# Row normalisation in a context attention pass: from VectorE to ScalarE, in slot 2 of a turn's last group

## The reference

```
def _layernorm(x, axis=-1, eps=1e-05):
    m = jnp.mean(x, axis=axis, keepdims=True)
    v = jnp.var(x, axis=axis, keepdims=True)
    return (x - m) / jnp.sqrt(v + eps)
...
q = _split_heads(Q @ Wq.T + bq, N_HEAD)          # Q = _layernorm(x); 512 rows, 16 heads of 32
k = _split_heads(K @ Wk.T + bk, N_HEAD)          # K = V = the context, 77 rows
score = jnp.einsum('bhqd,bhkd->bhqk', q, k) / jnp.sqrt(jnp.float32(d_k))
attn = jax.nn.softmax(score, axis=-1)
out = jnp.einsum('bhqk,bhkd->bhqd', attn, v)
...
x = x + jnp.tanh(g_xattn[1]) * (out @ Wo.T + bo)
```

## Time and profile before

| what | value |
|---|---|
| median of 3 runs | 2726.01 us (2723.91 to 2733.47) |
| the profiled execution | 2719.8 us, span 2718.0 us |
| mean granted TensorE clock of it | 0.944 |
| busy over the span: PE, DVE, ACT, POOL | 2356.2 (87%), 1419.5 (52%), 1028.4 (38%), 599.7 (22%) us |
| context attention pass in the span | about 1612 to 2024 us |
| one turn in its middle | 45.6 us |

### The profile page before, as it was taken

The page is one execution under the profiler, slowest core; times in us unless marked ns, Lnnn a source line. Parts: engine busy times, 40 slices in busy tenths (PEclk is TensorE's granted clock), DMA queues, the critical chain, the costliest instruction groups (busy, mean ns, idle before and its releaser), DMA issues. The chain is left out here.

```text
span 2718.0 us, 40799 instructions
## 1 busy us (share of the span) xinstructions
PE 2356.2 (87%) x16348; PEld 1549.0 (57%) x16348; DVE 1419.5 (52%) x1733; ACT 1028.4 (38%) x1185; POOL 599.7 (22%) x204
## 2 busy tenths in 40 slices
PE   7259999999999984799999857999968999999978
PEld 6235555555555542445444325666646888888756
DVE  4345565565565543567777647787745222222124
ACT  3324454454444441355555533444423111111111
POOL 0004654545554562000000002232320000000000
PEclk9679999999999986999999978999988999999989
DMA  7701011011010004111111021122224111111166
GB/s 239 181 33 38 16 46 41 11 44 31 24 45 10 14 13 132 32 48 58 51 46 47 17 86 53 67 83 70 68 93 144 42 44 44 45 44 48 45 234 261
DMA packets 104571, 182.56 MB, mean 67 GB/s; under 512 B 17252, under 2 KB 39780, under 8 KB 99358
## 3 DMA queue, kind: packets, MB, share of 16 engines
q1 hardware_dynamic: 100110, 172.84, 19.2%
q10 hardware_dynamic: 4368, 8.39, 0.8%
HBM read 122.07 MB, written 59.15 MB: 67 GB/s over the span
## 5 line engine op out<-in xcount | busy, mean ns | idle before, releaser
L976 DVE TENSOR_REDUCE att_mx<-att_sn 128x2 f32<-128x1024 f32 x256 | 313.6, 1225 | 169.1 <-PE att_sn L821 166.3
L733 POOL TENSOR_TENSOR att_es<-att_es,att_num 128x2048 f32<-128x2048 f32 x64 | 292.7, 4574 | 15.6 <-ACT att_num L904 9.3
L904 ACT ACTIVATE att_num<-att_st 128x2048 f32<-128x2048 f32 x128 | 240.6, 1879 | 141.0 <-PE att_st L809 81.0
L729 POOL TENSOR_TENSOR att_es<-att_num 128x2048 f32<-128x2048 f32 x32 | 145.9, 4559 | 370.7 <-PE att_pj L791 340.8
L2290 ACT ACTIVATE rec_ga<-rec_g,rec_bg 128x512 f32<-128x512 f32 x84 | 57.2, 689 | 312.0 <-PE rec_g L2189 312.0
L821 PE MATMUL att_sn<-att_kh,att_qh 32*128 32x512 f32 x512 | 127.6, 494 | 29.3 <-DVE att_mx L976 29.3
L1533 DVE TENSOR_TENSOR ffn_hs<-ffn_h,ffn_fb 128x1024 f32<-128x1024 f32 x64 | 78.0, 1219 | 115.9 <-PE ffn_h L1233 106.8
L1233 PE MATMUL ffn_h<-ffn_xqt,ffn_w 128*128 128x512 bf16 x512 | 125.1, 389 | 13.1 <-DVE ffn_hs L1533 13.1
L821 PEld LDWEIGHTS att_sn<-att_kh,att_qh 32*128 32x128 f32 x512 | 48.4, 185 | 148.2 <-DVE att_mx L976 110.9
L1840 POOL TENSOR_TENSOR xat_pr<-xat_e,xat_rd 128x1232 f32<-128x1232 f32 x32 | 73.1, 2283 | 241.8 <-DVE xat_rd L2026 235.0
L784 PE MATMUL att_pj<-att_num,att_v 128*32 128x512 f32 x1024 | 123.5, 601 | 1.0 <-issue 1.0
(11 more groups left out here) (375 smaller groups left out, 5859.6 us busy)
## 6 DMA issues: line engine op xcount, KB each, us to landing
att_x<-in_x SPq DMA_DIRECT2D x8, 1024.0 KB, 5.4
att_f<-in_fside_BxSxS SPq DMA_DIRECT2D x8, 1024.0 KB, 7.7
heads<-att_o SPq DMA_DIRECT2D x32, 256.0 KB
ffn_ol<-heads SPq DMA_DIRECT2D x8, 1024.0 KB, 5.3
ffn_x<-in_x SPq DMA_DIRECT2D x8, 1024.0 KB, 5.4
x<-ffn_xr SPq DMA_DIRECT2D x32, 256.0 KB, 2.0
xat_x<-x SPq DMA_DIRECT2D x8, 1024.0 KB, 5.2
xat_xr<-x SPq DMA_DIRECT2D x8, 1024.0 KB
```

The source lines that it names most:

```text
L729: pool.tensor_tensor(ES[:], E[0][:], E[1][:], ALU.add).then_inc(s_sum, 1)
L733: pool.tensor_tensor(ES[:], ES[:], E[k][:], ALU.add).then_inc(s_sum, 1)
L904: act.activation(E[k][:], st_ps[:], ACT.Exp, scale=SCALE).then_inc(s_exp, 1)
L976: dve.tensor_reduce(MX[c % 2][:, m // 2, 2 * DH * (m % 2):2 * DH * (m % 2) + DH + 1:DH], sn_ps[:], AX, ALU.max, negate=True).then_inc(s_ma ...
```

## The change

`ln.scale` of this pass goes from VectorE to ScalarE. ScalarE computes X times rstd plus shift, with scale and bias taken per partition. The bias, shift = -mean times rstd (4 columns), is made by VectorE. In the turns ScalarE's four instructions stand in group 3, slot 2, behind the job "q 2" and the copy of slot 2; VectorE's one instruction stands in group 3, slot 1. A new semaphore s_norm counts ScalarE's four; TensorE's "x" jobs and SyncE's loads of X wait for it in place of s_dve. Ahead of the turns ScalarE does rows 0 first of all and rows 1 behind the first three "q" copies.

```
+    NORM_SLOT = 2
...
+        shift = ps.sb("shift", [P, T])
+        ROWS_N = 2 * T + 2
+        s_norm = ps.sem("norm")
...
-                sp.wait_ge(s_dve, (i + 3) * ln.DVE_N)
+                sp.wait_ge(s_norm, (i + 3) * T)
                 load_x(i + 3)
...
                 if kind == "x":
-                    pe.wait_ge(s_dve, (b + 1) * ln.DVE_N)
+                    pe.wait_ge(s_norm, (b + 1) * T)
...
+            def normalised(b):
+                act.wait_ge(s_dve, b * ROWS_N + ROWS_N)
+                if not (isinstance(b, int) and b == 0):
+                    act.wait_ge(made["x"], b * C)
+                for t in range(T):
+                    act.activation(XN[:, t, :], X[:, t, :], ACT.Identity, bias=shift[:, t:t + 1],
+                                   scale=ln.rstd[:, t:t + 1]).then_inc(s_norm, 1)
...
                     if probabilities:
                         taken_out(*probabilities, j)
+                    if c == 3 and j == NORM_SLOT and not (isinstance(b, int) and b >= B - 2):
+                        normalised(b + 2)
 
             def ahead():
+                normalised(0)
                 for task in AHEAD:
                     job(-1, task)
+                normalised(1)
...
+            def normalise(b, part, first=False):
+
+                me = Steps(s_dve, b, ROWS_N)
+                if part == 0:
+                    dve.wait_ge(s_x, b * 16 + 16)
+                    ln.moments(dve, me)
+                else:
+                    me.done = 2 * T + 1
+                    dve.wait_ge(ln.s_rstd, b + 1)
+                    if not (isinstance(b, int) and b == 0):
+                        dve.wait_ge(s_norm, b * T)
+                    me.inc(dve.scalar_tensor_tensor(shift[:], ln.mv[:, :, 0], -1.0, ln.rstd[:], ALU.mult, ALU.mult))
...
-                    if not last and j == 3 and c in (1, 3):
+                    if not last and (c, j) in ((1, 3), (3, 1)):
                         normalise(b + 2, c // 2)
```

More of the change, by code:

```diff
@@ L1809, in _ @@
             load_values(0)
-            sp.wait_ge(s_dve, ln.DVE_N)
+            sp.wait_ge(s_norm, T)
             load_x(1)
@@ L1813, in _ @@
             sp.dma_start(XR[:], rows(x2_s, 0)).then_inc(s_xr, 16)
-            sp.wait_ge(s_dve, 2 * ln.DVE_N)
+            sp.wait_ge(s_norm, 2 * T)
             load_x(2)
@@ L1993, in _ @@
             dve.wait_ge(s_x, 16)
-            ln.rows(dve, 0, Steps(s_dve, 0, ln.DVE_N))
+            for part in range(2):
+                normalise(0, part)
             def job(turn, task):
@@ L2026, in sums @@
                 dve.reciprocal(RD[c % 2][:], SU[c % 2][:]).then_inc(s_rd, 1)
[L2028 to L2037, removed]
             def group(b, c):
```

## The result

The changed kernel takes 2753.7 us (median of 6, 2747.43 to 2760.45) against 2727.56 us for the kernel before (median of 6): a ratio of 1.0094, 95% interval 1.0071 to 1.0117. The forecast was 2749 us, +0.85%, in a range of 2736 to 2761 us.

What follows compares the result with a forecast made beforehand. TensorE was taken to set the pass's pace. A turn: +2.85 (stall) - 1.1 (VectorE in time) + 1.9 (clock) = +3.65 us; six turns +21.9, start +1.4, together +23.3 on 2726.0: 2749.3 us, range 2736 to 2761.

Steps and rivals of the forecast that it cites:

- The stall: Ahead of "att 2": ScalarE's four rows delay the slot 3 copy, so TensorE waits 2.85 us more a turn.
- The clock: Behind the new stall TensorE's clock falls to 0.50 in nearly every one of six turns, costing 1.9 us a turn.
- The rival in which the clock stays up: Rival: the clock mostly stays at 1.00 behind the stall, +11.9 us in all, 2737.9 us; chance 0.2.
- VectorE in time: With 8.09 us a turn removed from VectorE, TensorE's waits on it at the next turn's start shrink by 1.1 us.
- The start: Ahead of the turns: rows 0 on ScalarE add 0.5 us, rows 1 ahead of the table load 0.9 us; +1.4 us.
- The sum: Whole kernel: +3.65 us a turn, +21.9 for six turns, +1.4 at the start, together +23.3 us: 2749.3 us, +0.85%.
- Not slower, the relief outweighs: Rival: ScalarE's four rows fall into its waits and only VectorE's relief is left, -5 us, 2721 us; chance 0.06.

Runs made afterwards that it cites:

- e1: Changed kernel with twelve products of constant tiles put on TensorE into the wait ahead of "att 2", turns 1 to 6: 1.0027 of the kernel before.
- e2: Changed kernel with ScalarE's four rows in slot 1 of group 3 instead of slot 2: 0.9972 of the kernel before.
- e4: Changed kernel with two of ScalarE's four rows in slot 1 and two in slot 2 of group 3: 1.0052 of the kernel before.
- e3: Changed kernel with ScalarE's four rows in slot 3 of group 3, behind the last copy: 0.9983 of the kernel before.
- e6: Kernel before, with GpSimd's addition in group 3 waiting until VectorE has scaled that turn's rows, nothing moved to ScalarE: 0.9967 of the kernel before.
- e5: Kernel before, VectorE still scaling its rows, with four unread activations added on ScalarE in group 3 slot 2: 1.0090 of the kernel before.

## Why the prediction was right, point by point

- *The stall.* +2.85 us a turn forecast from the attention pass's own rows, 2.81 measured (e1 less e2), 3.76 us of waiting where about 3.8 us was said. The place decided, as argued: the same four instructions cost nothing in slot 1 and slot 3.
- *The clock.* 1.9 us a turn forecast, behind nearly every stall. It fell behind all six, and cost 1.53 and 3.10 us by turns, 2.3 on average: the term of the sum that was too small, by 0.4 us a turn. That it would fall was argued from the stall's being longer than any in the trace of before; e4 takes that ground away, since at 2.35 us, which is shorter than the 2.90 us that left the clock up, it fell behind five of six. The rule that the step quotes from the Trainium skill ("TensorE: Matmul & The Clock Gate", section "HAM oscillation — how this bites in real kernels") is one for waits between short stretches of work, and here a whole turn of 45.6 us goes from one stall to the next. So the fall behind every stall was forecast rightly, and what decides it stays open. The rival in which the clock stays up was right only in one turn of six in e4, at 2.35 us.
- *VectorE in time.* 1.1 us a turn forecast, 1.20 measured in e2, e3 and e6 (45.64 less 44.44). The amount held, its reason in the changed kernel did not: the step put it down to the 8.09 us removed from VectorE, and e5 shows that the stall itself covers them. That this term held in the sum of the changed kernel is in part luck. What is removed pays only where there is no stall.
- *The start.* +1.4 us forecast, as 0.5 and 0.9. Its two parts measure 0.4 us (from the end of VectorE's last instruction for the moments to TensorE's first transposes it is 4.47 us instead of 4.06) and 0.8 us, which is also what the prediction's own rows give (1659.7 less 1658.91).
- *The sum.* 6 x (2.81 - 1.20 + 2.3) + 1.2 = 24.7 us, where the medians show 26.1. Of it 0.4 us lies ahead of the first transposes, so that 24.3 compare with the 27.3 of the pass. The remaining 3.0 us of this one execution lie in the first turn (1.8) and in the last two (1.1), where the clock was low for 6.8 and 3.4 us longer than in the profile of before.
- *Not slower, the relief outweighs.* Its own condition, four rows that delay the slot 3 copy by less than 1.1 us, is what e2 and e3 set up, and they came out at 0.9972 and 0.9983.

## What to carry to other kernels

An engine that idles half of the time still has instructions that another engine stands waiting for; before work is moved onto it, look for the wait into which it fits, and put it there. Here one slot earlier turned +0.9% into -0.3%, and one slot later into -0.2%. And when an instruction is long because another engine runs beside it, it may be worth as much to move the neighbour by one wait as to move the work: here it was 0.9967 against 0.9972.

## What I had not expected of the hardware

A stall on TensorE costs more than its length: 2.81 us more of waiting brought 1.53 or 3.10 us of slower work behind it, and twelve products of no use in its place took that away. Stalls of one and the same 2.35 us had both outcomes in e4, so the length alone doesn't say whether the clock falls.
